# Projections moved into the lead of eight attentions, and the turned maxima moved ahead of the first products at group ends

## The chip, the cores and the metric

One core of a Trainium2 chip runs the whole program. The metric is the device time of one launch in microseconds (us); the kernel before was timed three times. PE is TensorE, DVE is VectorE, ACT is ScalarE, POOL is GpSimd.

## The reference, cut to what matters

A decoder of four layers works on x (2 sequences, 512 tokens, width 128) and a context of 77 tokens. The change touches its eight attentions. Each has the same core:

```
q, k, v = x @ Wq (+ bq), source @ Wk (+ bk), source @ Wv (+ bv)     # the source is x or the context
p = softmax(q @ k.T * scale [causal, or future keys only, in two of them], axis=-1)
out = p @ v
```

In the order of the program: layer 0 self-attention (16 heads of width 8, rotary done before), layer 0 cross (width 8, 77 keys), layer 1 cross (the same with biases), layer 1's causal attention (width 64, 4 key heads), layer 2 self-attention (width 8, with low-rank queries: a second product makes them from the first), layer 2 cross (width 64, 77 keys), layer 3 attention 1 (width 32, masked to future keys) and attention 2 (width 32, 77 keys). Between them stand norms, experts and feed-forward parts that the change leaves alone.

## The kernel before, in words

Every stage is a block; the engines meet at its end. An attention takes two kinds of block.

**The projections** run in `matmul_stream` (L212 is its matmul line): PE makes one product after another into the eight PSUM banks in turn, and ACT (L234, L235) and DVE (L245, L246) take turns to copy them to SBUF. In layer 1's causal attention only V is made so; its Q and K come from a block of their own with the rotary terms (L1380 to L1398). Layer 2's self-attention has two such streams, since the second reads what the first made.

**`row_attention`** is the attention itself. A group is one sequence and 128 / W heads that share the 128 partitions (W = 32: four heads; W = 64: two heads, called halved in the code). A round is one tile of keys of a group, so a group has four rounds with 512 keys and one round with 77. For each row of scores the maximum is needed before the exponential:

- `raw_scores` (L476): a first product of Q and K in bf16 for the maxima alone, into a ring of banks: three banks when heads are 8 wide, otherwise two. `reduce_max` on DVE (L602) reads it, and that frees the bank.
- `negmax` (L609, L610) makes the negative maxima of a group, `turn_negmax` (L488) transposes them on PE, again through a bank of the ring, and `move_negmax` (L615) copies them for PE to read.
- `scores` (L503, L507) is the float32 product with the turned maxima added to it. At the first round of a group PE waits for L615 before it. It goes to banks 2 to 5. ACT makes the exponentials from there (L704).
- `values` (L537), `sums` (L551, L557), `turn_sums` (L579) and `spread_inverses` (L587) follow a round or more behind. The last two also use the ring.

The ring is filled and emptied strictly in order: item n waits until item n - 2 or n - 3 was read. PE and DVE each walk a list written out by hand. In the round that ends a group the list before was, for PE: scores of this round, the first products `soon` for a later group, values of the round before, the turned maxima of the next group, sums, turned sums, first products `rest`, spread inverses. With W = 64 all first products are `soon`. For DVE it was: negmax, the maxima of `soon`, move_negmax, and so on.

**The lead** of an attention is what comes before its first round: the first products of the first group and of the first round of the second (20 of 512 columns in layer 0's self-attention), their maxima, and the turned maxima. Banks 2 to 5 and ACT are idle in it.

## Time and profile before

| | |
|---|---|
| median of 3 runs | 2001.85 us (2001.14 to 2003.67) |
| the profiled execution | 1997.6 us, span 1995.8 us |
| PE busy | 1566.4 us, 78% of the span |
| DVE busy | 1134.8 us, 57% |
| ACT busy | 610.3 us, 31% |
| mean granted clock of PE | 0.862 of 2.4 GHz |

No engine is busy throughout. PE's share is the largest, but it includes time at half clock (1.2 GHz), and a busy share says nothing of which wait ends last in one stage. So the rows below are read stage by stage: where a stream ends and the next block begins, which instruction a round waits for, and at which clock.

### The profile page before, as it was taken

What the parts mean: (1) busy time and instruction counts of PE and PEld (TensorE: products, weight loads), DVE (VectorE), ACT (ScalarE), POOL (GpSimd) and SP (SyncE); (2) the same over time, 40 slices, a digit from 0 to 9 for tenths busy, and PEclk for the clock granted to TensorE, in tenths of its full rate; (3) what the DMA queues carried; (4) which work ended last, traced back from release to release, by engine and by line L of the source; (5) the groups of instructions that cost most, each with busy time, mean ns of one, the idle gap of its engine ahead of it and who ended that gap; (6) DMA issues with size and microseconds to landing.
All of it is one profiled execution on the core that took longest, in us unless ns stands there. A gap on an engine that the chain in (4) does not pass through costs nothing. (4 is left out here: it accounts for less than half of the span.)

```text
span 1995.8 us, 23570 instructions
## 1 busy us (share of the span) xinstructions
PE 1566.4 (78%) x8740; PEld 718.1 (36%) x8740; DVE 1134.8 (57%) x2827; ACT 610.3 (31%) x839; POOL 131.8 (7%) x156
## 2 busy tenths in 40 slices
PE   1798659994666888885978997985988479994984
PEld 0332334441233433444433323352436223343342
DVE  5685544446966666644455854545454556744445
ACT  1265332223314023321432651411221124541331
POOL 1000000001000500000000000000000103321000
PEclk9799769996978999996997997886986778997687
DMA  4000000003000000000010000000010000000000
GB/s 187 0 2 1 1 1 0 0 0 124 0 1 1 21 22 2 1 1 1 0 75 18 1 1 0 1 1 1 0 63 0 1 0 1 1 1 1 1 1 11
DMA packets 4081, 27.37 MB, mean 14 GB/s; under 512 B 384, under 2 KB 2432, under 8 KB 2944
## 3 DMA queue, kind: packets, MB, share of 16 engines
q1 hardware_dynamic: 2912, 25.35, 3.2%
q8 instruction: 70, 1.15, 0.2%
q10 hardware_dynamic: 1056, 0.52, 0.1%
q14 instruction: 43, 0.35, 0.1%
HBM read 25.34 MB, written 0.52 MB: 13 GB/s over the span
## 5 line engine op out<-in xcount | busy, mean ns | idle before, releaser
L704 ACT ACTIVATE big<-banks 128x1024 f32<-128x1024 f32 (+2 forms) x320 | 294.2, 958 | 427.8 <-PE banks L507 260.2
L602 DVE TENSOR_REDUCE maxima<-banks 128x1 f32<-128x512 f32 (+4 forms) x640 | 362.5, 603 | 100.9 <-PE banks L476 94.2
L503 PE MATMUL banks<-big 32*128 32x512 f32 (+6 forms) x1280 | 259.5, 656 | 16.8 <-DVE negmaxT L615 16.4
L476 PE MATMUL banks<-big 32*128 32x77 bf16 (+6 forms) x1024 | 161.2, 306 | 30.3 <-DVE maxima L602 18.3
L537 PE MATMUL banks<-big,v_heads 128*9 128x512 f32 (+7 forms) x1024 | 164.3, 585 | 5.8 <-ACT heads_out L657 2.9
L342 POOL TENSOR_TENSOR rstd<-mean_var,minus_half 128x4 f32<-128x4 f32 x46 | 46.9, 1020 | 1645.8 <-DVE mean_var L317 1645.8
L1110 DVE TENSOR_TENSOR big<-big,banks 128x512 f32<-128x512 f32 (+1 forms) x88 | 60.5, 687 | 130.5 <-PE banks L1058 125.2
L1085 ACT ACTIVATE big<-banks 128x512 f32<-128x512 f32 (+1 forms) x120 | 71.7, 597 | 200.6 <-PE banks L1055 200.6
L1068 PE MATMUL banks<-big,moe_weights 128*128 128x512 f32 (+1 forms) x240 | 123.0, 593 | 2.8 <-DVE big L1107 1.5
L476 PEld LDWEIGHTS banks<-big 32*128 32x128 bf16 (+1 forms) x1024 | 58.0, 100 | 166.3 <-DVE maxima L602 102.9
L503 PEld LDWEIGHTS banks<-big 32*128 32x128 f32 (+3 forms) x1280 | 77.9, 187 | 79.6 <-ACT big L704 36.2
L507 PE MATMUL banks<-negmaxT,pick 32*128 32x512 bf16 (+6 forms) x640 | 97.2, 385 | 0.0
L1055 PE MATMUL banks<-xT,moe_weights 128*128 128x512 f32 x176 | 92.3, 606 | 3.4 <-PEq L1628 2.5
L1056 PE MATMUL banks<-xT,moe_weights 128*128 128x512 f32 x176 | 91.6, 603 | 0.0
L291 PE MATMUL banks<-ident,x 128*128 128x128 f32 x88 | 24.1, 428 | 70.7 <-DVE x L327 69.4
L212 PE MATMUL banks<-big,moe_weights 128*128 128x512 f32 x108 | 60.9, 721 | 13.1 <-PEq L1857 6.1
L291 PE MATMUL banks<-ident,normed 128*128 128x128 f32 x64 | 16.9, 416 | 61.0 <-DVE normed L327 42.9
L890 PE MATMUL banks<-moe_weights,big 128*128 128x128 f32 x464 | 58.2, 290 | 7.3 <-PEq L664 3.2
L1068 PEld LDWEIGHTS banks<-big,moe_weights 128*128 128x128 f32 (+1 forms) x240 | 45.5, 191 | 47.4 <-issue 28.5
L246 DVE COPY big<-banks 128x512 f32<-128x512 f32 x34 | 23.5, 692 | 66.1 <-PE banks L212 66.1
L352 ACT COPY xT<-banks 128x512 f32<-128x512 f32 x22 | 12.9, 587 | 157.0 <-PE banks L291 157.0
L890 PEld LDWEIGHTS banks<-moe_weights,big 128*128 128x128 f32 x464 | 57.0, 206 | 10.7 <-issue 10.7
(368 smaller groups left out, 2246.1 us busy)
## 6 DMA issues: line engine op xcount, KB each, us to landing
moe_weights<-in_moe SPq DMA_DIRECT2D x1, 4896.0 KB, 22.1
moe_weights<-in_moe SPq DMA_DIRECT2D x1, 4864.0 KB, 15.0
moe_weights<-in_moe SPq DMA_DIRECT2D x1, 3264.0 KB, 10.6
moe_weights<-in_l3x SPq DMA_DIRECT2D x1, 3072.0 KB, 10.2
late_weights<-in_l2x SPq DMA_DIRECT2D x1, 2048.0 KB, 8.1
moe_weights<-in_l SPq DMA_DIRECT2D x1, 1234.0 KB, 13.2
rows<-in_rows SPq DMA_DIRECT2D x1, 1152.0 KB, 8.1
late_weights<-in_turned SPq DMA_DIRECT2D x1, 1152.0 KB, 17.3
```

Source lines behind the costliest of these rows:

```text
L212: last = nc.tensor.matmul(bank(u), lhsT, rhs, start=(k == 0), stop=(k == len(products) - 1))
L476: last = nc.tensor.matmul(RING[n % NR][:, x * klen:x * klen + last_key(t)], q[rows, t * P:(t + 1) * P], ks[rows, 0:last_key(t)], start=Tru ...
L503: nc.tensor.matmul(SC[pair % 2][0:size, j % 2, n0:S], ks[rows, i * P:i * P + size], q[rows, n0:S], start=True, stop=False)
L507: last = nc.tensor.matmul(SC[pair % 2][0:size, j % 2, n0:S], c.pick[rows, 4 // HB * j, 0:size], c.NMT[rows, g % 2, n0:S], start=False, sto ...
L537: last = nc.tensor.matmul(out[:, n0:S], vop(b, HB * k + j, i), e[:, n0:S], start=first, stop=end)
L602: nc.vector.tensor_reduce(dst, src, AX_X, ALU.max).then_inc(ring_free.up(), 1)
L704: nc.scalar.activation(E[pair % NEP][0:size, :, n0:S], SC[pair % 2][0:size, :, n0:S], ACT.Exp, scale=scale).then_inc(exp_ready.up(), 1)
L890: last = c.nc.tensor.matmul(psum, srcT[:, i, t * P:(t + 1) * P], w[:, i * P:(i + 1) * P], start=(i == 0), stop=(i == k - 1))
L1055: nc.tensor.matmul(G[s % 2][0:m, :], w1, x, start=True, stop=True).then_inc(gate_ready.up(), 1)
L1056: last = nc.tensor.matmul(U[s % 2][0:m, :], w3, x, start=True, stop=True)
L1068: last = nc.tensor.matmul(ACC[:, :], w2, hid[0:m, s % 2, :], start=(k == 0), stop=(k == n - 1))
L1085: nc.scalar.activation(sg[0:m, s % 2, :], G[s % 2][0:m, :], func).then_inc(gated.up(), 1)
```

## The change

The projections leave their own blocks. `row_attention` is given them as a list, and PE makes them in the lead, in banks 2 to 5; ACT alone empties them. Before the first product of a group PE waits until the projections that it reads are copied (`needs`), and before the first scores until all are. A V bias is now added by a product of one row (ones by the bias) instead of by DVE. In the round that ends a group, PE makes the turned maxima before the first products `soon`, and DVE copies them before it reads those products.

The core of the diff (all eight call sites change alike; one stands for them):

```diff
+    def project_bank(n):
+        _, rows, cols = projections[n][:3]
+        return c.bank[2 + n % 4][0:rows, 0:cols]
+
+    def project(pe, n):
+        products, _, _, _, after = projections[n]
+        if n >= 4:
+            pe.wait_ge(project_free.sem, project_free.at(n - 3))
+        if after is not None:
+            pe.wait_ge(project_free.sem, project_free.at(after + 1))
+        for m, (lhsT, rhs) in enumerate(products):
+            last = nc.tensor.matmul(project_bank(n), lhsT, rhs, start=(m == 0), stop=(m == len(products) - 1))
+        last.then_inc(projected.up(), 1)
+
     def raw_scores(pe, u):
         (b, k), (j, tl) = groups[u // U], units[u % U]
+        if needs and u % U == 0:
+            pe.wait_ge(project_free.sem, project_free.at(needs[b, k]))
...
         @block.tensor
         def _(pe):
-            for u in range(min(U + per_round, NU)):
-                raw_scores(pe, u)
+            made, first = 0, 0
+            while first < U + per_round or made < len(projections):
+                wanted = needs[groups[first // U]] if needs and first < U + per_round else made + 1
+                while made < min(max(wanted, made + 1 if first else 0), len(projections)):
+                    project(pe, made)
+                    made += 1
+                for u in range(first, min(first + 2, U + per_round)):
+                    raw_scores(pe, u)
+                first += 2
             turn_negmax(pe, 0)
+            if projections:
+                pe.wait_ge(project_free.sem, project_free.at(len(projections)))
             for r in range(R + later):
                 soon, rest = ahead(r)
                 if r < R:
                     scores(pe, r)
-                for u in soon:
-                    raw_scores(pe, u)
+                if next_group(r) is None:
+                    for u in soon:
+                        raw_scores(pe, u)
                 if 0 <= r - 1 < R:
                     values(pe, r - 1)
                 if next_group(r) is not None:
                     turn_negmax(pe, next_group(r))
+                    for u in soon:
+                        raw_scores(pe, u)
                 if 0 <= r - 1 < R:
                     sums(pe, r - 1)
...
         @block.scalar
         def _(act):
+            for n, (_, _, _, empty, _) in enumerate(projections):
+                act.wait_ge(projected.sem, projected.at(n + 1))
+                empty(act, project_bank(n)).then_inc(project_free.up(), 1)
...
                 if next_group(r) is not None:
                     negmax(dve, next_group(r), n)
+                    move_negmax(dve, next_group(r))
                 for u in soon:
                     n = reduce_max(dve, u)
-                if next_group(r) is not None:
-                    move_negmax(dve, next_group(r))
...
+def tiles_of(c, w, src, dst, k, half, bias=None, after=None):
+
+    d = dst[:, k, half * S:(half + 1) * S]
+    return ([(w[:, k * P:(k + 1) * P], src[:, half * S:(half + 1) * S])], P, S, act_copy(c, d, bias=bias), after)
+
+
+def natural(c, srcT, w, dst, width, row=None):
+
+    n = srcT.shape[1]
+    products = [(srcT, w)] + ([] if row is None else [(c.ones[0:1, 0:n], row[0:1])])
+    return (products, n, w.shape[1], lambda act, bank: c.nc.scalar.copy(dst, bank.rearrange("p (h d) -> p h d", d=width)), None)
...
-    products = []
-    for k in range(4):
-        products += halves(c, lambda half, k=k: [(c.headmat[:, k * P:(k + 1) * P], c.q32[:, 0, half * S:(half + 1) * S])], P, Q[:, k])
-    matmul_stream(c, products)
     turn(c, keys.rearrange("p t i bl d -> p (t i) (bl d)"), NT * ST, P, K.rearrange("p k t -> p (k t)").unsqueeze(1))
-    attention_8(c, [P] * ST, 8.0 ** -0.5, chunked=True)
+    projections = [tiles_of(c, c.headmat, c.q32[:, 0], Q, k, half) for half in range(2) for k in range(4)]
+    attention_8(c, [P] * ST, 8.0 ** -0.5, chunked=True, projections=projections,
+                needs={(b, k): b * 4 + k + 1 for b in range(B) for k in range(4)})
```

How the instructions stand, in three places. First, PE's row in layer 0's self-attention, from the projections of Q (`big<-headmat`) to the first scores. Before (L212 the projections, L377 the keys turned, L476 the first products, L488 the turned maxima, L503 the scores):

```order
L204 UNCONDITIONAL_BRANCH
L212 MATMUL banks<-big,headmat 128x512 x8
L200 UNCONDITIONAL_BRANCH
L370 UNCONDITIONAL_BRANCH
L377 MATMUL banks<-ident,big 128x128 x32
L369 UNCONDITIONAL_BRANCH
L665 UNCONDITIONAL_BRANCH
L476 MATMUL banks<-big 128x512 x20
L488 MATMUL banks<-ident_bf,negmax 128x128 x4
L503 MATMUL banks<-big 128x512 x4
```

and now (L483 the projections, L496 the first products, L508 the turned maxima, L523 and L527 the scores):

```order
L685 UNCONDITIONAL_BRANCH
L483 MATMUL banks<-big,headmat 128x512
L496 MATMUL banks<-big 128x512 x2
L483 MATMUL banks<-big,headmat 128x512 x7
L496 MATMUL banks<-big 128x512 x18
L508 MATMUL banks<-ident_bf,negmax 128x128 x4
L523 MATMUL banks<-big 128x512 x4
```

One projection stands ahead of the first two first products, and the other seven stand in one piece behind them, ahead of the other eighteen. The other attentions have the same shape: what the first group needs, two first products (all that a W = 64 group has), then all remaining projections, then the remaining first products.

Second, PE's row at the first group end of the same attention (four rounds a group, four heads). Before:

```order
L476 MATMUL banks<-big 128x512 x2
L503 MATMUL banks<-big 128x512 x4
L507 MATMUL banks<-negmaxT,pick 128x512 x4
L476 MATMUL banks<-big 128x512 x2
L537 MATMUL banks<-big,v_heads 9x512 x4
L488 MATMUL banks<-ident_bf,negmax 128x128 x4
L476 MATMUL banks<-big 128x512 x2
L503 MATMUL banks<-big 128x512 x4
L507 MATMUL banks<-negmaxT,pick 128x512 x4
```

and now (L557 the values):

```order
L496 MATMUL banks<-big 128x512 x2
L523 MATMUL banks<-big 128x512 x4
L527 MATMUL banks<-negmaxT,pick 128x512 x4
L557 MATMUL banks<-big,v_heads 9x512 x4
L508 MATMUL banks<-ident_bf,negmax 128x128 x4
L496 MATMUL banks<-big 128x512 x4
L523 MATMUL banks<-big 128x512 x4
L527 MATMUL banks<-negmaxT,pick 128x512 x4
```

The two first products that stood between the scores and the values now stand behind the turned maxima, beside the two that were there already: four in one piece, ahead of the next group's scores.

Third, PE's row for two rounds in the middle of layer 2's cross attention (one round a group, two heads). Before (L551 the sums, L579 the turned sums, L587 the spread inverses):

```order
L476 MATMUL banks<-big 128x77 x8
L537 MATMUL banks<-big,v_heads 64x512 x2
L488 MATMUL banks<-ident_bf,negmax 128x128 x4
L551 MATMUL banks<-big,ones 32x512 x4
L579 MATMUL banks<-ident,heads_out 128x128 x4
L503 MATMUL banks<-big 77x512 x2
L507 MATMUL banks<-negmaxT,pick 77x512 x2
L476 MATMUL banks<-big 128x77 x8
L537 MATMUL banks<-big,v_heads 64x512 x2
L488 MATMUL banks<-ident_bf,negmax 128x128 x4
L587 MATMUL banks<-ident,inverses 128x128 x8
L503 MATMUL banks<-big 77x512 x2
```

and now (L571 the sums, L599 the turned sums, L607 the spread inverses):

```order
L557 MATMUL banks<-big,v_heads 64x512 x2
L508 MATMUL banks<-ident_bf,negmax 128x128 x4
L496 MATMUL banks<-big 128x77 x8
L571 MATMUL banks<-big,ones 32x512 x4
L599 MATMUL banks<-ident,heads_out 128x128 x4
L523 MATMUL banks<-big 77x512 x2
L527 MATMUL banks<-negmaxT,pick 77x512 x2
L557 MATMUL banks<-big,v_heads 64x512 x2
L508 MATMUL banks<-ident_bf,negmax 128x128 x4
L496 MATMUL banks<-big 128x77 x8
L607 MATMUL banks<-ident,inverses 128x128 x8
L523 MATMUL banks<-big 77x512 x2
```

The eight matmuls of two first products moved from behind the scores to between the turned maxima and the sums or the spread inverses.

## Rows read from the trace of the kernel before

**Rows 1.** Timeline, layer 0 self-attention: start us, us, engine, line, operation, [idle before <-releaser]
```profile
56.38 8.69 PE L212 MATMUL banks<-big,headmat 128*128 128x512 f32 x16 [1.05 <-PEq L369]
66.12 3.69 PE L377 MATMUL banks<-ident,big 128*128 128x128 f32 x32 [1.05 <-PEq L200]
...
71.40 9.59 DVE L602 TENSOR_REDUCE maxima<-banks 128x1 f32<-128x512 f32 x16
...
84.23 2.09 PE L503 MATMUL banks<-big 32*128 32x512 f32 x8 [0.85 <-DVE negmaxT L615]
```

**Rows 2.** Timeline, layer 0 cross attention, its last projections and its first scores
```profile
219.24 9.19 PE L212 MATMUL banks<-xT,late_weights 128*128 128x512 f32 x16
...
227.61 0.59 ACT L234 COPY big<-banks 128x512 f32<-128x512 f32 x1 [1.13 <-PE banks L212]
...
233.97 2.01 PE L503 MATMUL banks<-big 32*77 32x512 f32 x8 [0.63 <-DVE negmaxT L615]
```

**Rows 3.** Timeline, causal attention: its V stream, the rotary block, its first scores
```profile
651.09 6.57 PE L212 MATMUL banks<-moe_weights,big 128*128 128x256 f32 x16 [1.02 <-PEq L276]
...
658.37 1.10 PE L1380 MATMUL banks<-big,moe_weights 128*128 128x512 f32 x2 [0.72 <-PEq L200]
...
704.61 2.08 PE L503 MATMUL banks<-big 64*128 64x512 f32 x4 [0.52 <-DVE negmaxT L615]
```

**Rows 4.** Timeline, layer 0 self-attention, its first group end
```profile
99.41 0.42 DVE L615 COPY negmaxT<-banks 128x512 bf16<-128x512 bf16 x1
99.75 1.28 DVE L602 TENSOR_REDUCE maxima<-banks 128x1 f32<-128x512 f32 x2
...
99.89 1.15 PE L503 MATMUL banks<-big 32*128 32x512 f32 x8
```

**Rows 5.** Timeline, layer 0 cross attention, a round in its middle
```profile
254.98 0.66 PE L503 MATMUL banks<-big 32*77 32x512 f32 x3
...
255.34 0.85 DVE L602 TENSOR_REDUCE maxima<-banks 128x4 f32<-128x308 f32 x2
```

**Rows 6.** Timeline, causal attention, a middle group end, then its last
```profile
759.35 0.39 ACT L704 ACTIVATE big<-banks 128x256 f32<-128x256 f32 x1 [2.67 <-PE banks L516]
...
763.08 1.02 ACT L704 ACTIVATE big<-banks 128x1024 f32<-128x1024 f32 x1 [3.34 <-PE banks L516]
...
876.51 0.39 ACT L704 ACTIVATE big<-banks 128x256 f32<-128x256 f32 x1 [2.67 <-PE banks L516]
...
879.65 1.02 ACT L704 ACTIVATE big<-banks 128x1024 f32<-128x1024 f32 x1 [2.75 <-PE banks L516]
```

**Rows 7.** Timeline, layer 2 cross attention: last projections, first scores, then two round ends
```profile
1235.07 1.98 PE L212 MATMUL banks<-xT,late_weights 128*128 128x512 f32 x4
...
1241.35 1.99 PE L503 MATMUL banks<-big 64*77 64x512 f32 x4 [0.52 <-DVE negmaxT L615]
...
1264.05 0.33 PE L476 MATMUL banks<-big 64*128 64x77 bf16 x8
...
1265.65 1.06 PE L551 MATMUL banks<-big,ones 77*32 77x512 f32 x8
1265.76 0.42 DVE L615 COPY negmaxT<-banks 128x512 bf16<-128x512 bf16 x1 [0.50 <-PE banks L488]
...
1269.64 0.40 PE L488 MATMUL banks<-ident_bf,negmax 128*128 128x128 bf16 x4
...
1271.21 1.09 PE L503 MATMUL banks<-big 64*77 64x512 f32 x4
```

**Rows 8.** Busy time by stretch: bounds, length, PE, PEld, DVE, ACT, POOL, clock, DMA
```profile
740.00:870.00 130.00, 115.55 (x1026) 51.95 (x1024) 90.36 (x268) 43.94 (x68) 0.00 (x0) 1.00 0.00 1
1241.00:1261.00 20.00, 17.96 (x86) 5.71 (x86) 5.32 (x18) 4.92 (x7) 0.00 (x0) 0.50 0.00 0
1261.50:1300.00 38.50, 37.32 (x296) 15.48 (x293) 24.63 (x68) 16.82 (x24) 0.00 (x0) 1.00 0.01 1
1862.50:1895.00 32.50, 30.41 (x212) 11.28 (x213) 14.21 (x40) 10.96 (x14) 0.00 (x0) 0.50 0.00 1
```

More of the change, by code:

```diff
@@ L865, in keys @@
         return K[:, k, b * klen:(b + 1) * klen]
-    row_attention(c, key_tiles, 8, lambda b, k: Q[:, k, b * S:(b + 1) * S], keys, vop, scale, c.Y8)
+    row_attention(c, key_tiles, 8, lambda b, k: Q[:, k, b * S:(b + 1) * S], keys, vop, scale, c.Y8, projections=projections, needs=needs)
 def block_product(c, aT, bT, dst):
@@ L1018, in cross_attention_8 @@
 def cross_attention_8(c, wq, wk, wv, wo, bq, bk, bv, bo):
-    units, one = cross_kv(c, wk, wv, bk, bv)
-    Q, _ = heads_8(c, SK)
-    for k in range(4):
-        bias = None if bq is None else bq[:, k:k + 1]
-        units += halves(c, lambda half, k=k: [(wq[:, k * P:(k + 1) * P], c.XT[:, half * S:(half + 1) * S])], P, Q[:, k], bias=bias)
-    fill(c, one, 1.0)
-    matmul_stream(c, units)
-    attention_8(c, [SK], 8.0 ** -0.5)
+    ctxT = c.m("ctxT")[0:CTX]
+    Q, K = heads_8(c, SK)
+    v = c.VH[0:SK, 0:B * HEADS * 9].rearrange("p (b h e) -> p b h e", b=B, e=9)
+    fill(c, v[:, :, :, 8], 1.0)
+    col = lambda bias, k: None if bias is None else bias[:, k:k + 1]
+    projections = []
+    for k in range(4):
+        projections += [context_tile(c, wk, ctxT, K, k, bias=col(bk, k)), tiles_of(c, wq, c.XT, Q, k, 0, bias=col(bq, k))]
+    projections += [natural(c, ctxT[:, b * SK:(b + 1) * SK], wv, v[:, b, :, 0:8], 8, row=bv) for b in range(B)]
+    projections += [tiles_of(c, wq, c.XT, Q, k, 1, bias=col(bq, k)) for k in range(4)]
+    needs = {(0, k): 2 * k + 2 for k in range(4)} | {(1, k): 11 + k for k in range(4)}
+    attention_8(c, [SK], 8.0 ** -0.5, projections=projections, needs=needs)
     turn(c, c.Y8, NT, P, c.yT8)
@@ L1405, in layer1_ffn @@
     row_attention(c, [P] * ST, 64, lambda b, k: y[:, k, b * S:(b + 1) * S], lambda b, k: K[:, k % 2, b * S:(b + 1) * S],
-                  lambda b, h, i: V[:, b * ST + i, h % 4, 0:64], 0.125, y, mask="causal")
+                  lambda b, h, i: V[:, b * ST + i, h % 4, 0:64], 0.125, y, mask="causal",
+                  projections=[natural(c, nT[:, t * P:(t + 1) * P], c.m("wv"), V[:, t], 64) for t in range(NT)])
     yT = y
```

102 lines of the change are left out of this document (43 added, 59 removed).

## The prediction, made before the changed kernel ran

> **What bounds the kernel now.** I read the busy shares first: PE is busy 78% of the span, DVE 57%, ACT 31%. That asks for less PE work, but the change removes hardly any PE work; it moves it. So the stages have to be read one by one. The timelines of the attentions' starts come next [rows 1 to 3, 7]: a block of projections, a gap of 1.05 us until the next block's first matmul, then the lead, in which DVE reduces one first product after another and PE waits, until L503 starts once L615 has copied the turned maxima. The reader should see that in layer 0's self-attention [rows 1] 56.38 to 84.23 is spent ahead of the first scores, 16 matmuls of it in a block of their own, and that the 16 reductions of 9.59 us (0.60 each) set the rest. Then the timelines of group ends [rows 4 to 7]: the first scores of a group start after L615 and after whatever PE has in its row ahead of them. Last the busy time by stretch [rows 8]: the causal attention's loop runs at a granted clock of 1.00 although PE is busy only 115.55 of 130 us; layer 2's cross attention has its first 20 us at 0.50, with PE busy 17.96, and the 38.5 us behind them at 1.00, with PE busy 37.32; layer 3's attention 2 runs its stretch at 0.50 too. In these cross attentions PE's own row is the bound, so each matmul wait and the clock count in full.
>
> **The leads.** The change intends projections between first products. The order of PE's row shows less: what the first group needs, two first products, then all remaining projections in one piece. So DVE reduces two first products beside the projections and no more, a block boundary goes, and before the first of the first products PE waits for ACT's copy of what it reads.
>
> Layer 0 self: without its own block 66.12 − 56.38 = 9.74 us go [rows 1]. In the lead come back eight projections. Each stands in the trace as two matmuls, and at full clock these follow each other every 0.43 (the four of 1.98 us in rows 7, the last with a tail of some 0.26): 16 × 0.43 = 6.9, where the block took 8.69, since it began at half clock. I take 8.0: the 6.9, a tail of 0.4, and 0.7 for the copy that PE waits for (0.59 for 512 columns, the row of ACT in rows 2, and 0.1 to be seen). Hidden are two reductions of 0.60 and part of the zeroing before them, 1.6 together. That makes −9.74 + 8.0 − 1.6 = −3.3. Against it the half-clock beginning (8.69 − 6.9 = 1.8) moves onto the transposes of the keys, now first in that place, whose 32 matmuls took 3.69 us: +1.7. Net −1.6; the bounds are −3.3 (no cold beginning) and 0.
>
> Layer 0 cross [rows 2]: the stream's last matmul ends at 219.24 + 9.19 = 228.43. With the copy wait of 0.7 and two first products of 0.33 ahead (the width of the row at 1264.05 in rows 7) it ends at 229.46. The lead began 1.05 behind the stream's end, the gap of rows 1, and took 233.97 − 229.48 = 4.49; two reductions of 0.43 [rows 5] and the zeroing are done beside projections, so 3.3 are left: 232.75, which is −1.2. Layer 1 cross is the same with two added bias products (0.49 in all, two of about 0.25): −0.7. Layer 3's two attentions I take as layer 0's cross, −1.2 each. Layer 2's self-attention loses the gap between its two streams, but its V bias is now eight products of one row on PE instead of being part of DVE's copy: I take −0.5, between −1.2 and +0.8 (eight times 0.25 on top of −1.2).
>
> Causal [rows 3]: the V block, 658.37 − 651.09 = 7.28, goes. Its first part ran at half clock and warmed PE for the rotary block, which now starts cold: the V stream's 6.57 for 16 matmuls of 256 columns are 3.1 more than 16 × 0.215, half of 0.43. So +3.0. The lead gets the eight V products at full clock, 3.4, of which DVE's first two reductions, their masking and zeroing hide 0.9: +2.5. Net −1.8. Layer 2 cross [rows 7]: projections end at 1235.07 + 1.98 = 1237.05, now with copy wait and first products 1238.1; behind them stand two first products, the turned maxima and L615, 1.55 together: first scores at 1239.65 instead of 1241.35, −1.7.
>
> Sum of the leads: −1.6 − 1.2 − 0.7 − 1.8 − 0.5 − 1.7 − 1.2 − 1.2 = −9.9. ACT's table load for the exponential (three attentions) and its copies lie in the lead beside DVE; the last copy ends 0.7 behind the last projection and the first scores start 3.3 behind it [rows 2], so I cost them at nothing; without that cover a load or a late copy would delay the first exponential by itself, not the scores. DVE's copies leave it, but it was not the bound of the streams. SP's queue and the DMAs aren't touched.
>
> **The group ends.** With the turned maxima first, L615 comes earlier, but all `soon` products now stand between them and the next scores, and the ring lets product n start only once n − 2 or n − 3 is read.
> Width 8, four rounds: L615 ends at 99.83, scores start at 99.89 [rows 4]. The last of four first products now needs a reduction that starts only behind L615 and takes 0.6: scores at 100.5, +0.6. Six such ends in each of two attentions: 12 × 0.6 = +7.2. If the lost time is regained within the group's three other rounds, it is 0.
> Width 8, 77 keys [rows 5]: the same wait for one reduction of 0.43, in each of five rounds that have products left: about 0.4 each and 0.1, +2.2, in two attentions +4.4.
> Causal: here the products are two. Today negmax is followed by two reductions before L615 copies. The last group end has none, and shows what the order gives without them: from the exponential of the last round to the next group's 879.65 − 876.51 = 3.14, against 763.08 − 759.35 = 3.73 with them [rows 6]. So −0.57 × 13 ends and −0.3: −7.7. The two first products behind the copy need to be waited for; if their maxima then come late, it is 0.
> Layer 2 cross [rows 7], one group end in each round. In a round with L551 behind: everything is 0.33 earlier by the products moved; L615 then ends at 1265.85, the second product runs behind it, L551 starts at 1266.28 instead of 1265.65, +0.63. In a round with spread inverses, scores follow the turned maxima by 1271.21 − 1269.64 = 1.57; now the inverses need banks that two reductions must read first, 2.35, less 0.1: +0.68. Six and five such rounds and 0.2: +7.4. Nearest bounds: 0 (PE's row is as long) and +1.2 a round.
> Layer 3: attention 1 +0.15 × 6 = +0.9 (its DVE has time), attention 2 as layer 2's cross +0.65 × 5 = +3.3.
> Sum: 7.2 + 4.4 − 7.7 + 7.4 + 0.9 + 3.3 = +15.5, between −8 and +25.
>
> **The clock.** Layer 2's cross attention starts its loop at half clock, behind 1237.05 to 1241.35, in which PE had only short first products. The gap is now 1.55 us, and behind a stream at full clock. I take it that the clock stays at 2.4 GHz: of 17.96 us of PE [rows 8] half, 8.98, goes, less 0.7 where PE would then wait for copies: −8.25. The two width-8 cross attentions have a short stretch of the same kind behind their leads: −0.9 together. Attention 2 of layer 3 (30.41 of 32.5 us at 0.50) had its stream and lead with more first products; its gap shortens by 1.2 only, and I leave it as it is.
>
> In the Trainium skill, "TensorE: Matmul & The Clock Gate", section "A second HAM failure mode: psum-queue depth-cycling" says that small idle times of PE between groups of matmuls make the clock swing between its two levels. By that rule the new waits inside each round speak against this gain and could cost clock in loops that have it now, which is what rival 4 prices from rows. The trace does not bear it out so far: the causal loop with more idle time in it stays at 1.00 [rows 8].
>
> **Sum.** 1997.6 − 9.9 + 15.5 − 8.25 − 0.9 = 1994.05 for the profiled execution. The median of the runs is 4.25 above the profiled time of before, so 1998.3; I say 1998. From no change at all it differs by 3.6 us, and 0.2% (4 us) is about what a measurement of this kernel can tell from none.
>
> **Rivals.**
> 1. Slower: layer 2's cross attention still begins at half clock, since the wait for L615 ahead of its first scores remains. For it: attention 2 of layer 3 and this one both fell after leads. Against: the gap is a third. Place 1239.6 to 1259, price 8.25, so 2006.5; it decides from the point where less than half of that stretch is won. Chance 0.22.
> 2. Attention 2's loop stays at full clock as well, after a stretch that now runs without a boundary. Its 30.41 us of PE would be 15.2, but DVE's 14.21 and waits keep some: −10, so 1988. Chance 0.10.
> 3. The reductions that I charge at width 8 are regained inside the group, since DVE is busy for only 57% of the span: −11.6, so 1986.5. Chance 0.08.
> 4. The new waits bring the clock down in a loop that has it now. Layer 2's cross loop from 1261.5 on is busy 37.32 of 38.5 us at 1.00 and would double: half a loop is +18, so about 2016; or the reorder costs more than 25. Chance 0.10.
> 5. Leads and ends are both smaller than I say and cancel, no clock changes but the two small ones: 2001. Chance 0.08.
> That the change doesn't do what it says is already in the forecast: the projections are not interleaved. Were they, layer 0's lead alone would lose not 3.3 but the whole 8.0 under 9.59 us of reductions.
>
> **How the numbers follow.** Forecast 0.42, its own range 1995 to 2002. Faster by over 0.2% (below 1997.85) are 0.21 of the forecast, rivals 2 and 3 and 0.01 of the rest: 0.40. Slower (above 2005.85): 0.14 of rival 1, rival 4 and 0.02 of the forecast: 0.26. The rest, 0.34, is the same. The range: it takes in the forecast, rivals 1 and 5 and the near half of rivals 2 and 3; left out are 0.09 below 1990 and rival 4's 0.10 above 2008.5.
>
> **What would show it.** In the changed profile: layer 0's first scores 1.6 us earlier from its stage's start; the gap between L615's end and first scores 0.6 longer at width-8 ends; 3.15 between the causal pair of exponentials; rounds of layer 2's cross 0.6 longer at 1.00, and its first four rounds at 1.00 instead of 0.50. The prediction is wrong if that clock row reads 0.50, if another loop's reads below 1.00, or if the exponentials of a width-8 group are no further apart than before.

## The result, and the profile after

| | before | changed |
|---|---|---|
| median of 10 runs each, us | 2001.7 (1998.32 to 2003.67) | 2007.99 (2003.69 to 2008.91) |
| ratio to before, 95% interval | | 1.0027 (1.0017 to 1.0037) |
| profiled execution, us | 1997.6 | 2007.83, span 2006.0 |
| PE, DVE, ACT busy, us | 1566.4, 1134.8, 610.3 | 1586.1, 1095.4, 644.5 |
| mean granted clock | 0.862 | 0.869 |

The changed kernel is slower by 0.27%, and I had forecast it faster by 0.19%. The two profiled executions are 10.2 us apart, the medians 6.3: the execution profiled before lay 4 us under its own median. So the loss in the profile is to be read as 6 to 10 us.

The span was cut at each attention's first scores and at the end of its last exponential, by the timelines of both kernels. "Lead" is from the first projection of the attention (layer 0 self: before from its projections, at 56.38, now from the transposes of its keys, at 56.30; causal: from the block ahead of the rotary product, its V stream before) to the first scores, "loop" from there to the end of the last exponential.

| attention | lead before | lead changed | forecast | loop before | loop changed | forecast |
|---|---|---|---|---|---|---|
| layer 0 self | 27.85 | 28.03 | −1.6 | 108.09 | 109.62 | +3.6 |
| layer 0 cross | 17.91 | 19.89 | −1.2 | 27.44 | 29.15 | +1.8 |
| layer 1 cross | 18.24 | 25.02 | −0.7 | 27.44 | 38.87 | +1.8 |
| causal | 53.52 | 51.29 | −1.8 | 182.71 | 175.82 | −7.7 |
| layer 2 self | 35.03 | 37.35 | −0.5 | 108.32 | 109.48 | +3.6 |
| layer 2 cross | 31.98 | 31.87 | −1.7 | 69.52 | 68.38 | −0.9 |
| layer 3, attention 1 | 38.18 | 37.23 | −1.2 | 133.57 | 134.82 | +0.9 |
| layer 3, attention 2 | 20.47 | 20.95 | −1.2 | 50.10 | 45.76 | +3.3 |
| sum | 243.2 | 251.6 | −9.9 | 707.2 | 711.9 | +6.4 |

The loops came out at +4.7 where the steps give +6.4, the leads at +8.5 where I said −9.9. The rest of the program, which the change does not touch, is 3 us shorter. Against the forecast the leads are off by 18.4 us, the loops by 1.7 and the rest by 3.0, so the leads carry the error.

The first lead, in the timeline of the changed kernel (start, duration, engine, line; to be held against [rows 1]):

```profile
63.80 1.10 PE L483 MATMUL banks<-big,headmat 128*128 128x512 f32 x2 [1.05 <-PEq L369]
...
65.58 0.40 PE L496 MATMUL banks<-big 32*128 32x512 bf16 x2 [0.68 <-ACT big L234]
65.91 6.28 PE L483 MATMUL banks<-big,headmat 128*128 128x512 f32 x14
66.01 1.29 DVE L622 TENSOR_REDUCE maxima<-banks 128x1 f32<-128x512 f32 x2 [1.57 <-PE banks L496]
...
72.54 0.69 DVE L622 TENSOR_REDUCE maxima<-banks 128x1 f32<-128x512 f32 x1 [5.25 <-PE banks L496]
```

PE waits 0.68 for ACT's copy, DVE reduces two first products, and then it stands still for 5.25 us while the other seven projections pass. The third reduction starts at 72.54; before, with reductions from 71.40 on at 0.60 each, the third began at 72.6. That the projections are in one piece was right.

Next the granted clock in stretches that are one lead or one loop. The columns are bounds, length, busy time of PE, PEld, DVE, ACT and POOL, clock, DMA share, GB/s. Before: layer 0 cross's lead, layer 1 cross's lead and loop, then the loops of layer 2 cross and of layer 3's attention 2.

```profile
216.10:234.00 17.90, 14.68 (x68) 8.02 (x68) 7.65 (x19) 3.50 (x8) 0.00 (x0) 0.79 0.00 1
577.30:595.60 18.30, 15.01 (x68) 8.23 (x68) 7.88 (x19) 4.32 (x8) 0.00 (x0) 0.78 0.01 2
595.60:623.00 27.40, 26.50 (x296) 11.47 (x296) 17.66 (x54) 18.75 (x22) 0.00 (x0) 0.94 0.00 1
1241.40:1311.00 69.60, 66.56 (x450) 25.50 (x451) 35.71 (x100) 28.11 (x38) 0.00 (x0) 0.86 0.00 1
1866.00:1916.00 50.00, 47.70 (x361) 17.43 (x361) 20.57 (x57) 21.75 (x28) 0.00 (x0) 0.67 0.00 1
```

The same five in the changed kernel:

```profile
217.70:237.60 19.90, 17.22 (x66) 7.15 (x67) 4.60 (x14) 6.17 (x14) 0.00 (x0) 0.71 0.00 1
581.00:606.00 25.00, 22.34 (x68) 9.08 (x68) 4.66 (x13) 7.58 (x14) 0.00 (x0) 0.57 0.00 1
606.00:645.00 39.00, 37.21 (x296) 13.93 (x296) 17.64 (x55) 18.97 (x22) 0.00 (x0) 0.67 0.00 1
1257.20:1325.60 68.40, 63.86 (x449) 25.00 (x450) 35.59 (x100) 27.95 (x38) 0.00 (x0) 1.00 0.00 1
1879.20:1925.00 45.80, 42.74 (x362) 15.70 (x363) 20.52 (x55) 21.89 (x28) 0.00 (x0) 0.83 0.01 1
```

A granted clock between 0.50 and 1.00 is a mean over time at 1.2 and at 2.4 GHz, so the time at half clock is length × 2 × (1 − clock). In layer 0 cross's lead that was 7.5 us and is 11.5; in layer 1 cross's lead 8.1 and 21.5. PE does half as much in it, so half of the difference is lost: 2.0 and 6.7 us, as much as these two leads grew (1.98 and 6.78). Layer 1's cross loop fell to 0.67, layer 2's rose to 1.00 as forecast, attention 2's rose to 0.83.

The group ends. Layer 0 self, answering to [rows 4]; then two of the causal attention's exponentials [rows 6]; then two round ends of layer 2 cross [rows 7]:

```profile
97.52 1.94 ACT L739 ACTIVATE big<-banks 128x1024 f32<-128x1024 f32 x2 [1.24 <-PE banks L527]
...
99.01 0.42 DVE L635 COPY negmaxT<-banks 128x512 bf16<-128x512 bf16 x1 [1.36 <-PE banks L508]
99.35 3.10 DVE L622 TENSOR_REDUCE maxima<-banks 128x1 f32<-128x512 f32 x5
...
100.19 1.15 PE L523 MATMUL banks<-big 32*128 32x512 f32 x8
...
101.57 1.02 ACT L739 ACTIVATE big<-banks 128x1024 f32<-128x1024 f32 x1 [2.12 <-PE banks L527]
...
776.29 0.38 ACT L739 ACTIVATE big<-banks 128x256 f32<-128x256 f32 x1 [2.67 <-PE banks L536]
...
779.53 1.02 ACT L739 ACTIVATE big<-banks 128x1024 f32<-128x1024 f32 x1 [2.85 <-PE banks L536]
...
1277.81 0.40 PE L508 MATMUL banks<-ident_bf,negmax 128*128 128x128 bf16 x4
...
1280.27 1.09 PE L523 MATMUL banks<-big 64*77 64x512 f32 x4
```

Scores follow the end of L635, the copy of the turned maxima, by 0.76 us (99.43 to 100.19) where they followed L615 by 0.06. The causal pair is 3.24 apart, 3.73 before. In layer 2 cross, scores follow the turned maxima by 2.46 with spread inverses between them, 1.57 before.

### The profile page after: what moved, and what is told of

Same layout as the page of the kernel before. It is cut to its first block and busy times, and to the rows that moved or that the text cites. A ratio compares the mean times of both kernels' runs of the same rounds, so it can differ in the third digit from the quotient of the medians.

```text
span 2006.0 us, 23583 instructions
## 1 busy us (share of the span) xinstructions
PE 1586.1 (79%) x8760; PEld 721.9 (36%) x8760; DVE 1095.4 (55%) x2760; ACT 644.5 (32%) x906; POOL 131.8 (7%) x156
## 5 line engine op out<-in xcount | busy, mean ns | idle before, releaser
L523 PE MATMUL banks<-big 32*128 32x512 f32 (+6 forms) x1280 | 256.0, 646 | 7.6 <-DVE negmaxT L635 7.2
L496 PE MATMUL banks<-big 32*128 32x77 bf16 (+6 forms) x1024 | 168.1, 303 | 38.8 <-DVE maxima L622 17.8
L557 PE MATMUL banks<-big,v_heads 128*9 128x512 f32 (+7 forms) x1024 | 163.1, 584 | 5.9 <-ACT heads_out L677 2.9
L496 PEld LDWEIGHTS banks<-big 32*128 32x128 bf16 (+1 forms) x1024 | 58.9, 98 | 170.7 <-DVE maxima L622 93.3
L523 PEld LDWEIGHTS banks<-big 32*128 32x128 f32 (+3 forms) x1280 | 78.8, 184 | 62.3 <-ACT big L739 36.1
L527 PE MATMUL banks<-negmaxT,pick 32*128 32x512 bf16 (+6 forms) x640 | 98.3, 382 | 0.0
L635 DVE COPY negmaxT<-banks 128x512 bf16<-128x512 bf16 x80 | 33.9, 424 | 85.8 <-PE banks L508 85.8
L234 ACT COPY big<-banks 128x512 f32<-128x512 f32 (+1 forms) x82 | 42.9, 528 | 63.5 <-PE banks L483 58.1
L352 ACT COPY xT<-banks 128x512 f32<-128x512 f32 x22 | 12.9, 586 | 153.0 <-PE banks L291 153.0
## 6 DMA issues: line engine op xcount, KB each, us to landing
moe_weights<-in_l SPq DMA_DIRECT2D x1, 1234.0 KB, 12.9
late_weights<-in_turned SPq DMA_DIRECT2D x1, 1152.0 KB, 16.8
```

Source lines behind the costliest of these rows:

```text
L496: last = nc.tensor.matmul(RING[n % NR][:, x * klen:x * klen + last_key(t)], q[rows, t * P:(t + 1) * P], ks[rows, 0:last_key(t)], start=Tru ...
L523: nc.tensor.matmul(SC[pair % 2][0:size, j % 2, n0:S], ks[rows, i * P:i * P + size], q[rows, n0:S], start=True, stop=False)
L527: last = nc.tensor.matmul(SC[pair % 2][0:size, j % 2, n0:S], c.pick[rows, 4 // HB * j, 0:size], c.NMT[rows, g % 2, n0:S], start=False, sto ...
L557: last = nc.tensor.matmul(out[:, n0:S], vop(b, HB * k + j, i), e[:, n0:S], start=first, stop=end)
```

## The experiments

Each ratio is to the kernel before, run on the same chip beside it; its median was 2002.8 to 2003.1 in those jobs.

| kernel | median us | ratio, 95% interval |
|---|---|---|
| changed, again | 2008.07 | 1.0019 (1.0009 to 1.0029) |
| leads only | 2007.91 | 1.0026 (1.0015 to 1.0037) |
| ends only | 2002.92 | 1.0006 (0.9992 to 1.0020) |
| interleaved | 1985.4 | 0.9898 (0.9882 to 0.9915) |
| inter_causal | 1956.06 | 0.9762 (0.9749 to 0.9775) |
| inter_causal_kfirst | 1943.07 | 0.9681 (0.9663 to 0.9699) |
| after_kfirst | 2000.1 | 0.9972 (0.9956 to 0.9988) |
| before_warm | 1990.33 | 0.9945 (0.9926 to 0.9963) |
| after_late | 2003.11 | 0.9991 (0.9973 to 1.0008) |
| late_first | 1941.73 | 0.9694 (0.9673 to 0.9714) |
| late_first_warm | 1932.93 | 0.9657 (0.9633 to 0.9681) |
| causal_old | 1941.06 | 0.9696 (0.9669 to 0.9723) |

Loops of the profiled executions, in us, cut as above:

| kernel | L0 self | L0 cross | L1 cross | causal | L2 self | L2 cross | L3 a1 | L3 a2 |
|---|---|---|---|---|---|---|---|---|
| changed, again | 109.49 | 29.14 | 37.86 | 175.83 | 109.50 | 68.37 | 134.82 | 45.75 |
| leads only | 107.45 | 26.31 | 29.82 | 183.22 | 107.43 | 61.25 | 132.44 | 50.12 |
| ends only | 109.47 | 30.26 | 36.47 | 176.47 | 110.35 | 69.70 | 134.59 | 45.97 |
| interleaved | 109.50 | 29.14 | 29.14 | 174.44 | 107.38 | 68.38 | 132.12 | 39.56 |
| inter_causal | 107.70 | 26.32 | 26.32 | 174.39 | 105.27 | 61.28 | 131.20 | 35.99 |
| after_kfirst | 109.56 | 36.48 | 37.87 | 175.87 | 109.49 | 69.71 | 134.65 | 40.75 |
| before_warm | 108.07 | 27.43 | 27.43 | 182.70 | 108.27 | 61.33 | 133.78 | 35.98 |
| late_first_warm | 105.29 | 26.32 | 26.32 | 174.46 | 105.30 | 61.31 | 129.87 | 35.98 |

Leads, in us, cut as above (the causal one not cut):

| kernel | L0 self | L0 cross | L1 cross | L2 self | L2 cross | L3 a1 | L3 a2 |
|---|---|---|---|---|---|---|---|
| changed, again | 27.08 | 22.76 | 20.79 | 37.30 | 31.83 | 37.23 | 20.95 |
| interleaved | 23.03 | 21.17 | 23.87 | 34.38 | 35.74 | 31.43 | 23.70 |
| inter_causal | 23.79 | 19.17 | 23.04 | 34.39 | 31.99 | 31.34 | 23.88 |
| inter_causal_kfirst | 24.11 | 20.04 | 18.19 | 33.82 | 29.98 | 31.34 | 18.06 |
| after_kfirst | 27.92 | 19.07 | 19.44 | 37.32 | 27.99 | 39.27 | 19.87 |
| after_late | 27.50 | 18.28 | 23.39 | 37.49 | 29.64 | 39.28 | 24.44 |
| late_first | 23.27 | 15.39 | 16.20 | 34.39 | 25.82 | 32.88 | 16.75 |

**The changed kernel again.** No edit.

> The changed kernel once more, for a second profiled execution. Theory A (the clock's fall in layer 1's cross loop belongs to this order of work): that loop, 38.9 us in the first profile and 27.4 before, is again near 39 us, and layer 2's cross loop again starts at 1.00. Rival B (which loop falls is decided anew in each execution): it is back near 28 us here, or another attention is slow instead. Time 2004 to 2009 us under both.

Theory A held: layer 1's cross loop is 37.86 us, layer 2's again starts at full clock. What does vary from one execution to the next is which lead pays: layer 0's cross lead took 22.76 instead of 19.89, layer 1's 20.79 instead of 25.02. Their sum was 44.9 in the first profile and is 43.6 here, against 36.2 before. One such lead in one profile can therefore be 3 to 4 us off by itself, and the sum of the two says more.

**Leads only**, the group ends as before:

```diff
-                if next_group(r) is None:
-                    for u in soon:
-                        raw_scores(pe, u)
+                for u in soon:
+                    raw_scores(pe, u)
...
                     turn_negmax(pe, next_group(r))
-                    for u in soon:
-                        raw_scores(pe, u)
```

(and L635 back behind the maxima on DVE).

> The changed kernel with the group ends as before (first products soon ahead of the turned maxima, DVE's copy behind their maxima); only the leads differ from the kernel before. If my sizes of the ends hold (+15.5 us in all, of it -7.7 in the causal loop): about 1992 us, with the causal loop back at 182.7 and the width-8 loops at 108. Rival (the leads cost the time, through projections at half clock, and the ends are near nothing in sum): 2004 to 2008 us.

The rival held on the time, 2007.91, but not on the reason: the ends are not near nothing. The eight loops are 13.9 us shorter than in the changed kernel, and the stretches ahead of the first scores 12.9 longer; 6.9 of it lie between layer 1's cross loop and the causal scores, where no code differs and the clock is 0.73 instead of 0.88. Two stretches of it, layer 1's and layer 2's cross loops:

```profile
603.70:633.50 29.80, 29.11 (x296) 12.65 (x296) 17.63 (x53) 18.85 (x22) 0.00 (x0) 0.83 0.00 1
1259.30:1320.50 61.20, 58.20 (x449) 23.42 (x450) 35.66 (x100) 27.90 (x37) 0.00 (x0) 1.00 0.00 1
```

This kernel and the changed one both run layer 2's cross loop at 1.00, so 68.38 − 61.25 = +7.1 us is what the new order costs there (forecast +7.4), and 69.52 − 61.25 = 8.3 is what the clock gave (forecast 8.25). The causal loop is 183.22 against 175.82: −7.4. Layer 3's attention 2, with the new lead and the old order, took 50.12 us at 0.67, as before: its lead brought its clock nothing.

**Ends only**, the kernel before with the new order:

> The kernel before with only the group ends changed (turned maxima ahead of the first products soon). My sizes: +15.5 us, so about 2017 us. What the loops of the changed kernel's profile read (+1.5, +1.7, -6.9, +1.2, +1.3 and the clock apart): 2001 us, within 3. Layer 1's cross loop stays at 27 to 29 us if its fall came from the lead, and is near 39 if it came from the loop's order.

2002.92 is the second number of the expectation, not my +15.5. Yet the sizes were near: at equal clock (below) they add to +14.4. Here three loops changed their clock, with the leads as they were: layer 2's cross took 69.70 us, where 61.3 + 7.1 = 68.4 would be the price at full clock, attention 2 won 4.1, and layer 1's cross lost 9.0. Layer 2's first, then layer 1's:

```profile
1246.64:1250.64 4.00, 3.74 (x21) 1.43 (x23) 1.20 (x5) 1.02 (x1) 0.00 (x0) 0.63 0.00 0
1250.64:1316.34 65.70, 61.41 (x431) 23.83 (x428) 34.47 (x97) 26.91 (x37) 0.00 (x0) 1.00 0.00 1
...
598.40:634.90 36.50, 34.70 (x296) 13.10 (x296) 17.64 (x54) 18.97 (x22) 0.00 (x0) 0.73 0.00 1
```

Behind the same lead layer 2's loop still begins at half clock, but it is back at 1.00 after some 3 us, where it took 19 with the old order. So the order of the rounds decides too how long a loop stays down, and not always for the worse: by length × 2 × (1 − clock), with the old leads, the half clock in layer 2's cross loop went from 19.5 to 2.8 us and in attention 2's from 33 to 17, while in layer 1's cross it rose from 3 to 20. Layer 1's loop took 26.3 to 29.8 us with the old ends, and with the new ones 36.5 to 38.9 in all but `interleaved` (29.1, at 1.00) and after_late (34.1); so the new order alone does not bring its fall in every case.

**Interleaved**, the changed kernel with the lead's loop mended:

```diff
-                while made < min(max(wanted, made + 1 if first else 0), len(projections)):
+                goal = min(max(wanted, made + 1 if first else 0), len(projections))
+                while made < goal:
```

> The changed kernel with the lead's loop mended, so that one projection stands behind every two first products as long as there are first products. Theory A (the projections in one piece are what kept the leads from gaining): layer 0's first scores 5 to 6 us earlier than in the changed kernel (84.3), as much in layer 2's self-attention and layer 3's first, in sum -12 to -18 us, so 1990 to 1996 us. Rival (what the leads lose is the clock's, since PE has the projections at half clock between waits for DVE): less than 5 us better, and some leads longer.

Theory A held, and the gain of 22 us is more than the 12 to 18 that it said. The bound in the old loop was computed anew after each projection, so it ran to the end of the list. Now, in the timeline of layer 0's lead:

```profile
64.67 0.40 PE L496 MATMUL banks<-big 32*128 32x512 bf16 x2 [0.68 <-ACT big L234]
64.99 1.12 PE L483 MATMUL banks<-big,headmat 128*128 128x512 f32 x2
65.10 10.99 DVE L622 TENSOR_REDUCE maxima<-banks 128x1 f32<-128x512 f32 x16 [1.57 <-PE banks L496]
...
79.42 1.24 PE L523 MATMUL banks<-big 32*128 32x512 f32 x4 [0.94 <-DVE negmaxT L635]
```

DVE runs through 16 reductions without the 5.25 us gap. The three attentions with 512 keys and long leads gained 5.0, 3.0 and 5.8 us on the changed kernel. The leads on 77 keys did not gain (layer 2's: 35.74 against 31.87). More came through the clock: layer 1's cross loop ran at 1.00 (29.14 us), and attention 2's loop, also at 1.00, was 6.2 us shorter.

**inter_causal**, interleaved and the new order only where `mask == 'causal'`:

```diff
+                ahead_of_turn = mask == 'causal'
-                if next_group(r) is None:
+                if next_group(r) is None or not ahead_of_turn:
```

(and the same for the turned maxima and DVE).

> The mended lead of 'interleaved', and the turned maxima ahead of the first products in the causal attention alone; the seven other attentions have their group ends as before. From the loops read so far (width 8 with four rounds +1.1 to 2.1, width 8 with 77 keys +2.8, layer 2's cross +7.1, layer 3's first +2.4 with the change) they should give back about 15 to 17 us of 'interleaved' (1985.4): 1969 us. Rival: as between the changed kernel and the one with its leads alone, shorter loops are paid back through the clock, and it stays within 5 us of 1985.

1956.06, 29 us better than interleaved where 15 to 17 were expected. Against interleaved, with both at full clock, the loops of layer 0 and 1 cross are 2.8 us shorter each, layer 2's self 2.1, layer 2's cross 7.1, attention 2's 3.6; at 0.99 in both attention 1's is 0.9 shorter, and at 0.96 in both layer 0's self 1.8. The loops add up to 21.2; most of what is left is in two leads, layer 2's cross (−3.8) and layer 0's (−2.0).

**Order of the projections on 77 keys.** All of K first, on inter_causal and on the changed kernel:

```diff
-    for k in range(4):
-        projections += [context_tile(c, wk, ctxT, K, k, bias=col(bk, k)), tiles_of(c, wq, c.XT, Q, k, 0, bias=col(bq, k))]
+    projections += [context_tile(c, wk, ctxT, K, k, bias=col(bk, k)) for k in range(4)]
+    projections += [tiles_of(c, wq, c.XT, Q, k, 0, bias=col(bq, k)) for k in range(4)]
```

(the other two alike).

> As inter_causal, but in the attentions on the 77 keys the projections of K (154 columns, in two of the three from 64 rows) are all made before the projections of Q, as in the kernel before, instead of one K before each Q. Theory A (the alternation of small and large products keeps PE at half clock in these leads): the leads of layers 0 and 1 cross come back towards 18 us from stream's start to first scores, 3 to 5 us less each, so 8 us better than inter_causal. Rival (the first group waits for five projections instead of two, and nothing else changes): 2 to 4 us worse.

> The changed kernel with that order of projections alone. Theory A: layer 0's cross lead (19.9 and 22.8 us in two profiles, 17.9 before) is 17 to 18, layer 1's (25.0, 20.8 against 18.2) 18 to 19, and the whole 2000 to 2003 us. Rival (the waits for ACT's copies and for the first products, not the alternation): leads stay above 20 us, time 2006 to 2009 us.

Both whole times speak for theory A: 13 us better where it said 8, and 2000.1 where it said 2000 to 2003. The leads of the changed kernel with it, 19.07 and 19.44, are shorter than its 19.9 to 25.0 but above the 17 to 19 of theory A. Attention by attention it is half right: layer 0's lead did not clearly shorten (20.04 against 19.17 in inter_causal, 19.07 against 19.89 and 22.76 in the changed kernel), those of layer 1 (18.19, 19.44), layer 2 (29.98, 27.99) and attention 2 (18.06, 19.87) did, by 1.1 to 5.8 us. In after_kfirst two cross loops stayed long at half clock, layer 0's for the first time (36.48).

**Where the first products stand.** after_late puts all projections ahead of them in the changed kernel, late_first puts them among the last three on inter_causal_kfirst:

```diff
             made, first = 0, 0
+            if nkt == 1:
+                while made < len(projections) - 3:      # after_late: - 0
+                    project(pe, made)
+                    made += 1
```

> The changed kernel with one difference: in the four attentions on the 77 keys all projections come first and the first products behind them, as the kernel before has them, but still in one block and with ACT's copies alone. Theory A (the early first products and the wait for ACT's copy keep PE at half clock for longer in these leads): the leads of layers 0 and 1 cross come to 17 to 18 us from the first projection to the first scores (19.9 to 22.8 and 20.8 to 25.0 in the changed kernel, 17.9 and 18.2 before), and 3 to 6 us of the whole go. Rival (the alternation of K and Q or the phase of the clock): they stay above 19.5.

> On top of inter_causal_kfirst (1943.1), in those four attentions the first products stand only among the last three projections. Theory A: leads of layers 0 and 1 cross 16 to 17 us (20.0 and 18.2 there), layer 2's 28.5 (30.0), whole 1936 to 1939 us. Rival (the first products early are worth more as work beside DVE than the clock they cost): 1943 to 1948.

In after_late the whole came down by 5 us as theory A says, and layer 0's lead to 18.28, near its 17 to 18; layer 1's stayed at 23.39 as the rival says, with this clock:

```profile
217.20:235.40 18.20, 16.08 (x64) 6.78 (x64) 4.49 (x13) 6.06 (x14) 0.00 (x0) 0.78 0.00 1
580.00:603.40 23.40, 21.23 (x68) 8.81 (x68) 4.49 (x13) 7.58 (x14) 0.00 (x0) 0.64 0.00 1
```

Removing one cause alone is not enough: that kernel still alternates K and Q. With both removed, late_first has the shortest leads of the kernels without added products:

```profile
210.90:226.30 15.40, 14.37 (x66) 6.91 (x66) 4.78 (x14) 6.15 (x14) 0.00 (x0) 0.78 0.00 1
569.50:585.70 16.20, 15.16 (x72) 7.30 (x72) 4.81 (x14) 7.58 (x14) 0.00 (x0) 0.80 0.01 2
```

The four leads take 12.1 us less than in inter_causal_kfirst, but the whole gained nothing that the runs can tell: the medians are 1.3 apart, theory A's 1936 to 1939 was missed, and two of inter_causal_kfirst's five runs (1933.7 and 1934.7) lie below all of late_first's (1941.4 to 1943.7). In the profiles attention 2's loop fell back to half clock at its start (41.40 us instead of 35.97), and +4.0 us came between layer 1's cross loop and the causal first scores, where nothing was edited.

**Warm leads.** before_warm adds to the kernel before, in two attentions, products whose result is never read:

```diff
+            def keep_warm(count):
+                for x in range(count if warm else 0):
+                    nc.tensor.matmul(c.bank[2][:, x % 4 * P:(x % 4 + 1) * P], c.ident[:], c.ident[:], start=True, stop=True)
...
                 raw_scores(pe, u)
+                if u % 2:
+                    keep_warm(8)
             turn_negmax(pe, 0)
+            keep_warm(6)
```

> The kernel before, and in the leads of layer 2's cross attention and layer 3's attention 2 PE makes small products of the identity (128 columns, about 0.12 us each) where it waits for DVE: eight behind every second first product and six behind the turned maxima, into a bank that nothing reads. If the idle lead is what brings the half clock of these two loops: both begin at 1.00, 69.5 us become about 61.3 and 50.1 about 40, with 1 us lost to the added products: 1985 us. Rival (the clock falls by something further back or by the loop itself): within 3 us of 2001.9.

Held: both loops ran at 1.00, 69.52 became 61.33 and 50.10 became 35.98, 22.3 us together, and filling the waits of the two leads was the only edit:

```profile
1244.40:1305.70 61.30, 58.28 (x450) 23.43 (x450) 35.53 (x99) 27.89 (x37) 0.00 (x0) 1.00 0.01 1
1868.10:1904.10 36.00, 33.55 (x363) 14.03 (x363) 19.81 (x54) 21.88 (x28) 0.00 (x0) 1.00 0.01 2
```

The leads themselves grew by 2.9 and 5.4 us, more than the 1 us expected: there were 22 and 38 added products, and eight of them took 2.05 us with their tail (from 1238.56), some 0.25 each and not the 0.12 of the expectation. The profiled execution took 1985.4 us; two more runs took 1985 to 1986, the other three 1994 to 1998, and of those no trace was kept. The median, 1990.33, lies between them.

late_first_warm does it in every lead of late_first, with four and eight:

> As late_first, and small products of the identity in every lead where only DVE works: four behind each two first products that have no projection left beside them, eight behind the turned maxima. Loops that still begin at half clock (layer 0's self attention, 1.5 to 3 us of it) should begin at 1.00: 3 to 8 us less than late_first. Rival (the leads that remain are short enough already): 1 to 3 us more, for the added products delay the first scores.

8.8 us better than late_first, a little more than the 3 to 8 expected. Layer 0's self loop lost its half clock (107.46 to 105.29), attention 2's too (41.40 to 35.98):

```profile
80.20:185.50 105.30, 102.04 (x797) 32.10 (x796) 76.91 (x143) 65.37 (x71) 0.00 (x0) 1.00 0.00 1
1815.90:1851.90 36.00, 33.55 (x363) 14.02 (x363) 19.80 (x54) 21.88 (x28) 0.00 (x0) 1.00 0.01 2
```

At 1932.93 us, 0.9657 of before, it has the lowest median here and beats both kernels.

**causal_old**, that kernel with the causal group ends as before as well:

> late_first_warm (1932.9) with the group ends of the causal attention as before too, so that no group end is changed any more. If the turned maxima ahead of the two first products are worth there what the loops show (182.7 before, 174.4 to 175.8 with them): the causal loop goes to 181 to 183 us and the whole to 1939 to 1942. Rival (its gain is given back through the clock behind it): within 3 us of 1932.9.

1941.06, and the causal loop 181.40 against 174.46, both at 1.00; all other loops agree within 0.02 us. That part of the change is worth 7 us by itself.

## Why the prediction was wrong

**The group ends: right in sum, by sizes that partly cancelled.** At equal clock, from the pairs above: width 8 with four rounds +2.05 and +2.1 (leads only against the changed kernel at 0.96, inter_causal against interleaved at 1.00; forecast +3.6 each, since of the 0.7 lost at each of six ends, 4.2 in all, half is regained within the group, so that rival 3 is half true there), width 8 on 77 keys +2.8 each (29.14 − 26.32; forecast 2.2), causal −6.9 (174.46 − 181.40; −7.7), layer 2 cross +7.1 (+7.4), layer 3's attention 1 +0.9 (132.12 − 131.20; +0.9), attention 2 +3.6 (39.56 − 35.99; +3.3). Together +14.4, where I had +15.5.

**The clock: one half right, one missing.** Layer 2's cross loop at 1.00 for 8.3 us was right, so rival 1 did not come true. Three kernels bear on its reason. before_warm shows that the loop does not fall when the waits of its lead are filled, and leads only, that the new lead is enough, as I had argued. But ends only won nearly all of it (half clock 19.5 to 2.8 us) with the old lead and its gap, so the shorter gap was enough and not needed. Rival 2 came true in part: attention 2's loop is 4.3 us shorter though its new order costs 3.6, so about 7.9 came from the clock. Its reason, the lead, was wrong: leads only has that lead and took 50.12 us, ends only has the old one and took 45.97. Rival 4 came true in another place than I priced it: not layer 2's loop fell but layer 1's, which is 11.4 us longer, 2.8 by the order and 8.6 by the clock. My last paragraph had named another loop's row below 1.00 as a sign of being wrong, and layer 1's 0.67 is that sign. Gains and losses of clock inside these loops, −8.3 − 1.1 (layer 0 cross) − 7.9 + 8.6 = −8.7, and −1.1 in the others, again come near the −9.15 of the forecast, by luck and not by its steps.

**The step that failed: the sum of the leads**, −9.9 forecast, +8.5 in the profile. Its working took the projections at the clock that they had in their own block, and put the cost of mixing them with first products at one wait for a copy. Two of the eight terms were within half a us (causal −2.2 for −1.8, attention 1 −1.0 for −1.2). What the others missed:
- Layer 0 and 1 cross (−1.9 forecast, +8.8 in the first profile, +7.4 in the second): PE was at half clock for 33 us of these two leads instead of 15.6, which is 8.7 us of time; the other 2.0 of the miss were not taken apart. The alternation of K and Q and the first products with their copy wait in the middle of the projections keep it there. The sum of the two leads shows it: 42.2 to 45.0 us in the five profiles with both (the changed kernel twice, leads only, interleaved, inter_causal), 38.2 and 38.5 with K first, 41.7 with the first products late, 31.6 with both removed (late_first). Of kernels with the changed group ends, the changed one had 33 and 29 us of these leads at half clock, after_kfirst 22, after_late 25; late_first had 13. Layer 2's cross lead and attention 2's missed by 1.6 and 1.7 us, and shortened from 31.9 to 25.8 and from 21.0 to 16.8 with both removed.
- Layer 2 self (−0.5, +2.3): a V bias as a product of one row costs PE 0.41 us (from 1073.64 to 1074.05 in the changed kernel's timeline, below), not 0.25. Eight of them are 3.3 us, and the −0.5 held only 0.7 for them on top of −1.2: −1.2 + 3.3 = +2.1, near the +2.3 measured. The clock is 1.00 there.

```profile
1073.64 0.48 PE L483 MATMUL banks<-rows,ones 1*128 1x128 f32 x2
1074.05 0.49 PE L483 MATMUL banks<-mid_weights,xT 128*128 128x128 f32 x2
1074.47 0.48 PE L483 MATMUL banks<-rows,ones 1*128 1x128 f32 x2
```

- Layer 0 self (−1.6, +0.2): the key transposes beginning at half clock took 6.45 us (56.30 to 62.75) where they had taken 3.69, +2.8 and not +1.7; 0.6 more went into the eight projections (7.0 net of two reductions, not 6.4). That the projections are in one piece was read from the order and priced rightly; what it cost against the intended interleaving, 22 us of the whole, I had put at under 5 in one lead and not worked out for the others.

Layer 1's cross loop ran at 0.67 with the added waits, while layer 2's cross loop with 7 us of them stayed at 1.00. The rule of the Trainium skill weighed ahead of the sum ("TensorE: Matmul & The Clock Gate", section "A second HAM failure mode: psum-queue depth-cycling") has micro-idles between groups of matmuls make the clock swing between its levels. Neither loop shows such a swing: layer 2's stayed up, and layer 1's was down from its first scores at 606.05 and came up once, in the middle of rounds of one and the same order:

```profile
629.00:632.00 3.00, 3.00 (x24) 0.85 (x20) 1.63 (x6) 1.33 (x2) 0.00 (x0) 0.50 0.00 0
632.00:635.00 3.00, 2.66 (x40) 1.41 (x36) 1.85 (x6) 1.21 (x3) 0.00 (x0) 1.00 0.00 0
```

My argument from the causal loop, 1.00 with more idle time, did not carry over to layer 1's. Why one loop stays down and the other doesn't was not settled, nor why layer 0's cross loop stayed down in after_kfirst alone. That the moment at which a loop starts plays a part is not excluded: causal_old moved the loops of layers 2 and 3 by some 9 us with nothing else changed in them, and all stayed at 1.00, but its leads are warm; no such pair exists with waits in the leads.

The sign of the result hung on clock in the leads that the forecast took as unchanged: the 8.7 us of layer 0 and 1 cross alone are more than twice the 3.6 us that I forecast as gain. The row of the V stream in [rows 3] and the projections in [rows 1] begin at half clock; a change that puts short products and a wait into such a beginning needed a bound on the slow side for all of it being longer. The bounds that I gave for the leads ended at 0 in layer 0's self-attention and at +0.8 in layer 2's, and the cross leads had none.

## What to carry to other kernels

Read the order of the queue before the comments on what it should be: one bound computed inside a loop instead of ahead of it turned an interleaving into a block, and mending it moved the time from 1.0027 to 0.9898 of before, in part through the clock of loops behind the leads. When work is moved into a stretch in which PE waits for another engine, look up the granted clock of that stretch and of what follows. Here small products in the waits and large ones kept together were worth more than they cost (22.3 us in two loops for 8.3 in their leads), and the same reorder paid in one loop (7 us in the causal attention) and cost in seven others at equal clock.

## What the runs showed of the hardware

Two loops that start behind a lead of short products and waits spent 19.5 and 33 us at 1.2 GHz although PE was busy 90% of that time or more (PE 17.96 of 20 us at 0.50 [rows 8]). Products on the identity in the leads, 22 and 38 of 128 columns, removed it: 61.33 instead of 69.52 us and 35.98 instead of 50.10. Another order of the rounds behind the same lead cut 19.5 us at half clock to 2.8. At equal clock and with equal code a loop repeats within 0.1 us over kernels and executions (26.30 to 26.32, 61.25 to 61.33, 35.97 to 35.99), so what varies between profiled executions of this program is mostly where it runs at half clock. In layer 2's self-attention a product of one row by 128 float32 columns took PE as long in its queue at 1.00 (0.41 us) as one of 128 rows (0.42, from 1074.05 to 1074.47).
